# A gated state-space layer and a ternary feed-forward on one core: the prologue and the first units in another order, the dt projection in three row groups

## The reference, cut to what matters

```python
# x: (4, 512, 512); ctx: (4, 512, 256); 512 inner channels, 16 states, dt rank 16
xp  = einsum('bld,ed->bel', ctx, in_proj_w)
u   = silu(causal_conv4(xp, conv_w) + conv_b)
dt_low, B, C = split(einsum('bdl,ed->bel', u, x_proj_w), [16, 32])
dt  = softplus(dt_proj_w @ dt_low + dt_proj_b)
for each time l:                       # 16 states for each channel
    state = state * exp(dt * A) + dt * u * B[l]
    y     = sum_n(state * C[l])
x = x + tanh(g_x) * ((y + D * u) * silu(layernorm(x)))
# feed-forward, 2048 hidden, weights rounded to {-1, 0, 1} by scale 1 / mean|w|
h = silu(bitlinear(layernorm(x), w_gate)) * bitlinear(.., w_up)
x = x + tanh(g_ffn) * bitlinear(h, w_down)
```

## Time and profile before

| | |
|---|---|
| median of 3 runs | 621.03 us (620.51 to 621.07) |
| span of the profiled execution | 617.3 us |
| VectorE busy | 557.0 us, 90% |
| TensorE busy | 520.0 us, 84% |
| ScalarE busy | 519.0 us, 84% |
| GpSimd busy | 508.1 us, 82% |
| mean granted TensorE clock | 0.972 |
| moved by DMA | 64.25 MB |

### The profile page before, as it was taken

How to read it: one execution, slowest core, us unless ns; L and a number is a source line. 1 busy time by engine, 2 the same in 40 slices (tenths; PEclk the granted TensorE clock), 3 DMA queues, 4 the chain that set the end, 5 groups by cost and what they waited for, 6 DMA issues and landing times. The chain is left out here.

```text
span 617.3 us, 9751 instructions
## 1 busy us (share of the span) xinstructions
PE 520.0 (84%) x3254; PEld 363.1 (59%) x3254; DVE 557.0 (90%) x766; ACT 519.0 (84%) x796; POOL 508.1 (82%) x286
## 2 busy tenths in 40 slices
...
DMA packets 30420, 64.25 MB, mean 104 GB/s; under 512 B 3729, under 2 KB 11921, under 8 KB 27554
## 3 DMA queue, kind: packets, MB, share of 16 engines
...
...
## 5 line engine op out<-in xcount | busy, mean ns | idle before, releaser
L850 POOL TENSOR_TENSOR area_s<-area_s,b_bc 128x1024 f32<-128x1024 f32 x117 | 275.0, 2363 | 13.8 <-DVE u_all L1454 9.2
L483 PE MATMUL pY<-ident,area_s 128*128 128x128 f32 x532 | 87.6, 290 | 56.6 <-DVE area_s L1462 56.6
L552 PE MATMUL pG<-wq_gu,area_f 128*128 128x512 fp8e4 x448 | 107.9, 379 | 4.0 <-ACT area_f L1052 2.9
L1454 DVE TENSOR_TENSOR_SCAN area_s<-pA,area_s 128x512 f32<-128x512 f32 x88 | 105.2, 1207 | 5.1 <-ACT pA L1107 4.4
L483 PEld LDWEIGHTS pY<-ident,area_s 128*128 128x128 f32 x532 | 61.6, 146 | 78.0 <-DVE area_s L1462 70.5
L1107 ACT ACTIVATE pA<-dt_all,a_neg 128x512 f32<-128x512 f32 x145 | 97.7, 682 | 10.7 <-DVE area_s L1454 5.9
L842 POOL TENSOR_TENSOR u_all<-u_all 128x1024 f32<-128x1024 f32 x44 | 103.9, 2361 | 0.2 <-DMA u_all<-bc_rows 0.2
L1462 DVE TENSOR_TENSOR area_s<-area_s,pC 128x512 f32<-128x512 f32 x133 | 87.9, 664 | 0.8 <-DVE area_s L1454 0.5
L477 PE MATMUL pC<-ident,xdT 128*128 128x128 f32 x532 | 83.2, 283 | 3.6 <-DVE area_s L1462 2.3
L477 PEld LDWEIGHTS pC<-ident,xdT 128*128 128x128 f32 x532 | 64.3, 143 | 8.9 <-DVE area_s L1462 7.4
L552 PEld LDWEIGHTS pG<-wq_gu,area_f 128*128 128x128 bf16 x448 | 41.7, 98 | 47.1 <-ACT area_f L1052 3.9
...
## 6 DMA issues: line engine op xcount, KB each, us to landing
...
b_bc<-w_gate SPq DMA_DIRECT2D x1, 4096.0 KB, 14.5
dt_all<-x SPq DMA_DIRECT2D x1, 4096.0 KB, 24.8
area_f<-w_up SPq DMA_DIRECT2D x1, 4096.0 KB, 34.2
area_f<-w_down SPq DMA_DIRECT2D x1, 4096.0 KB, 14.4
...
```

Source lines behind the costliest of these rows:

```text
L483: mm = pe.matmul(pY[:, k * P:(k + 1) * P], src[:, k * P:(k + 1) * P], ident[:, :], is_transpose=True, start=(first and k == 0), stop=(last ...
L552: mm = pe.matmul(bank, xqT[t % 2][:, k, :], wq_gu[:, k, m, c * GW:(c + 1) * GW], start=(k == 0), stop=(k == NT - 1))
L850: gp.tensor_tensor(db[c % NDB], du[s % 2].rearrange("p (a l) -> p a l", a=1).to_broadcast([P, CH, L]), b_bc[:, CH * c:CH * c + CH, :], ALU ...
L1454: dve.tensor_tensor_scan(h, at, dbu, 0.0, ALU.mult, ALU.add).then_inc(S["s_scan"], 1)
```

## The change

The dt rows and their weights are laid out three times, at partitions 0, 32 and 96, and B and C move to partitions 64 to 95. `dt_proj(i)` then multiplies only 17 partitions, in the row group of its block. The projections use six banks in place of four. TensorE starts with ten transposes of the identity. All five programs get another order: TensorE makes projections 8 and 9 ahead of `x_proj(0)`, and 12 to 15 in one go. w_gate's chunks go to other engines: GpSimd rounds 0 and 1, VectorE 2 and 3 (`w_round`); ScalarE takes the signs of 0, 2 and 3, the last two in unit 0, and chunk 1 goes through `w_clip` and `w_ternary`. The sums of |w_up| move from VectorE's prologue to ScalarE's unit 0; the further steps of w_up and w_down each stand some states later, up to two signs of w_down in unit 4. The z statistics are handled as 4 and 12 columns. The diff's core:

```diff
-NPROJ = 64
-BROW = 32
+DT_AT = (0, 32, 96)
+BC_AT = 64
...
-px = [pA[:, 0, :], pA[:, 1, :], pC[:, 0, :], pC[:, 1, :]]
-pv = [pG[0][:, :], pG[1][:, :]] + px
...
+px = [pA[:, 0, :], pA[:, 1, :], pC[:, 0, :], pC[:, 1, :], pG[0][:, :], pG[1][:, :]]
+pv = px[4:] + px[:4]
...
-sp.dma_start(w_xp_sb[:, :, 0:RANK], w_xp[:, 0:RANK].rearrange("(t p) n -> p t n", p=P)).then_inc(S["c_w"], 16)
...
-sp.dma_start(w_dt_sb[0:RANK, :], w_dt).then_inc(S["c_w"], 16)
-sp.dma_start(w_dt_sb[RANK:RANK + 1, :], b_dt.rearrange("(a n) -> a n", a=1)).then_inc(S["c_w"], 16)
...
+sp.dma_start(w_xp_sb[:, :, 0:RANK], w_xp[:, 0:RANK].rearrange("(t p) n -> p t n", p=P)).then_inc(S["c_xp"], 16)
...
+for at in DT_AT:
+    sp.dma_start(w_dt_sb[at:at + RANK, :], w_dt).then_inc(S["c_w"], 16)
+    sp.dma_start(w_dt_sb[at + RANK:at + RANK + 1, :], b_dt.rearrange("(a n) -> a n", a=1)).then_inc(S["c_w"], 16)
...
 sp.dma_start(dt_all[:, :, :], x.rearrange("b (t p) f -> p (b t) f", p=P)).then_inc(S["c_x"], 16)
-sp.dma_start(stage[1].rearrange("p (k f) -> p k f", k=NT), w_up.rearrange("(k p) f -> p k f", p=P)).then_inc(S["c_g1"], 16)
-
...
 store_u(1)
+sp.dma_start(stage[1].rearrange("p (k f) -> p k f", k=NT), w_up.rearrange("(k p) f -> p k f", p=P)).then_inc(S["c_g1"], 16)
 store_bc(1)
 store_u(2)
-store_bc(2)
-sp.wait_ge(S["k_p3"], NW)
+sp.wait_ge(S["k_p3"], 1)
 sp.wait_ge(S["c_bst0"], 16)
 load_b(0, (0,))
+store_bc(2)
 store_u(3)
-load_b(0, (1,))
 sp.wait_ge(S["k_conv"], UNITS)
...
 load_z(1)
+sp.wait_ge(S["k_t3"], 1)
+load_b(0, (1,))
+store_bc(3)
 load_x(0)
-load_b(0, (2, 3))
-store_bc(3)
-load_x(1)
-
...
 load_c(0)
+sp.wait_ge(S["k_p3"], 2)
+load_b(0, (2,))
+sp.wait_ge(S["k_p3"], NW - 1)
+load_b(0, (3,))
+load_x(1)
 for b in range(1, BATCH):
...
-sp.wait_ge(S["k_p3"], 2 * NW)
+sp.wait_ge(S["k_p3"], 2 * NW - 1)
 sp.dma_start(stage[2].rearrange("p (k d) -> p k d", k=FK), w_down.rearrange("(k p) d -> p k d", p=P)).then_inc(S["c_g2"], 16)
...
-    past(pe, S["k_tap"], i - 3)
+    past(pe, S["k_tap"], i - 5)
...
-        mm = pe.matmul(px[i % 4], w_in_sb[:, k, t * P:(t + 1) * P], ctx_sb[:, b, k, :], start=(k == 0), stop=(k == KC - 1))
+        mm = pe.matmul(px[i % 6], w_in_sb[:, k, t * P:(t + 1) * P], ctx_sb[:, b, k, :], start=(k == 0), stop=(k == KC - 1))
...
-    if m < 2:
-        pe.wait_ge(S["k_abv"], NW + NW * m)
+    if m == 0:
+        pe.wait_ge(S["k_abv"], NW)
...
-        pe.wait_ge(S["k_abs"], NW)
+        pe.wait_ge(S["k_abs"], NW * m)
...
 def dt_proj(i):
     b, t = i // NT, i % NT
     pe.wait_ge(S["k_rows"], b + 1)
-    if i >= 2:
-
-        pe.wait_ge(S["k_tap"], min(UNITS - NT + i - 1, UNITS))
+    if i < 6:
+        pe.wait_ge(S["k_tap"], UNITS - 4 + i - i % 2)
     past(pe, S["k_dt"], i - 5)
-    pe.matmul(pv[i % 6], w_dt_sb[:, t * P:(t + 1) * P], rows[b], start=True, stop=True).then_inc(S["k_v"], 1)
-
+
+    at = DT_AT[t % 3]
+    pe.matmul(pv[i % 6], w_dt_sb[at:at + RANK + 1, t * P:(t + 1) * P], rows[b][at:at + RANK + 1, :],
+              start=True, stop=True).then_inc(S["k_v"], 1)
+
+pe.wait_ge(S["k_const"], 6)
+for _ in range(WARM):
+    pe.transpose(pT[:, 0:P], ident[:, :], ident[:, :])
 pe.wait_ge(S["c_in"], 16)
-for i in range(2 * NT):
+for i in range(10):
     project(i)
-pe.wait_ge(S["k_const"], 8)
-pe.wait_ge(S["c_w"], 7 * 16)
+pe.wait_ge(S["c_w"], 10 * 16)
+pe.wait_ge(S["k_cp"], 2)
 x_proj(0)
-project(8)
-project(9)
-rows_transpose(0)
 project(10)
 project(11)
-dt_proj(0)
-dt_proj(1)
+rows_transpose(0)
+for i in range(12, UNITS):
+    project(i)
 x_proj(1)
 w_total(0)
-project(12)
-project(13)
+x_proj(2)
 rows_transpose(1)
-project(14)
-project(15)
-x_proj(2)
-dt_proj(2)
-dt_proj(3)
+for i in range(NT):
+    dt_proj(i)
 rows_transpose(2)
-dt_proj(4)
-dt_proj(5)
 x_proj(3)
-for i in range(6, 3 * NT):
+for i in range(NT, 3 * NT):
     dt_proj(i)
 rows_transpose(3)
 for i in range(3 * NT, UNITS):
...
+gp.wait_ge(S["k_const"], 5)
...
+for i, at in enumerate(DT_AT):
+    gp.wait_ge(S["k_const"], 6 + i)
...
+gp.wait_ge(S["k_const"], 10)
...
+gp.wait_ge(S["c_xp"], 16)
+for at in DT_AT[1:]:
+    gp.tensor_copy(w_xp_sb[:, :, at:at + RANK], w_xp_sb[:, :, 0:RANK]).then_inc(S["k_cp"], 1)
...
-conv_sums(0, 10)
+conv_sums(0, 12)
...
-conv_sums(10, 12)
+conv_sums(12, UNITS)
...
-conv_sums(12, 14)
-w_round(2)
-conv_sums(14, UNITS)
-w_round(3)
-w_clip(3)
+w_clip(1)
...
+def z_roots(first, last, done):
...
+    gp.wait_ge(S["k_ag"], last)
...
+z_roots(0, NT, 0)
...
-gp.wait_ge(S["k_st"], 2 * UNITS)
...
+z_roots(NT, UNITS, 4)
...
-        if n in (1, 3, 5, 7):
+        if s == 0 and n == CH * pooled(s)[0] + 2:
+            times_c(s, 0)
+            times_b(s, NDB)
+            times_b(s, NDB + 1)
+        if n in (1, 3, 5, 7) and (s > 0 or n > 3):
...
-        if n == CH * pooled(s)[0] + 2:
+        if s > 0 and n == CH * pooled(s)[0] + 2:
...
-    act.wait_ge(S["k_p1"], NW * m + c + 1)
+    if m == 0 and c > 1:
+        act.wait_ge(S["k_p2"], c - 1)
+    else:
+        act.wait_ge(S["k_p1"], 2 + NW * (m - 1) + c + 1 if m else c + 1)
...
     if i:
         silu(i - 2)
         silu(i - 1)
-act.wait_ge(S["k_const"], 9)
-rows_out(0)
 conv_start(8)
 conv_start(9)
 silu(6)
 silu(7)
-act.wait_ge(S["c_w"], 7 * 16)
-act.activation(tgate[:, :], g_raw[:, :], ACT.Tanh).then_inc(S["k_a"], 1)
+act.wait_ge(S["k_const"], 10)
+rows_out(0)
 conv_start(10)
 conv_start(11)
 silu(8)
 silu(9)
-rows_out(1)
+act.wait_ge(S["c_w"], 10 * 16)
+act.activation(tgate[:, :], g_raw[:, :], ACT.Tanh).then_inc(S["k_a"], 1)
 conv_start(12)
 conv_start(13)
 silu(10)
 silu(11)
 conv_start(14)
 conv_start(15)
+rows_out(1)
+silu(12)
+silu(13)
 w_sign(0, 0)
 rows_out(2)
-silu(12)
-silu(13)
-w_sign(0, 1)
 silu(14)
 silu(15)
-w_sign(0, 2)
-for i in range(3):
+for i in range(NT):
     softplus(i)
 rows_out(3)
-for i in range(3, UNITS):
+for i in range(NT, UNITS):
     softplus(i)
 act.wait_ge(S["k_dt"], UNITS)
 act.wait_ge(S["k_a"], 2)
...
+        act.wait_ge(S["k_zs"], 8)
...
-    if s == 0 and n >= 4 and n % 2 == 0 and n < 4 + 2 * NW:
-        w_scale(1, n // 2 - 2)
-    if s == 1 and n % 2 == 0 and n < 2 * NW:
-        w_sign(1, n // 2)
-    if s == 2 and n % 2 == 1 and n < 1 + 2 * NW:
-        if n == 1:
+    if s == 0 and n in (0, 1):
+        w_sign(0, 2 + n)
+    if s == 0 and n in (5, 7, 11, 13):
+        if n == 5:
+            act.wait_ge(S["c_g1"], 16)
+        w_abs(1, (5, 7, 11, 13).index(n))
+    if s == 1 and n in (2, 4, 6, 8):
+        w_scale(1, n // 2 - 1)
+    if s == 1 and n in (10, 13, 15) or s == 2 and n == 1:
+        w_sign(1, (10, 13, 15, 1).index(n))
+    if s == 2 and n in (11, 13, 15) or s == 3 and n == 1:
+        if n == 11:
...
-        w_abs(2, n // 2)
-    if s == 3 and n % 2 == 0 and n < 2 * NW:
-        w_scale(2, n // 2)
-    if s == 3 and n in (8, 10, 12):
-        w_sign(2, 7 - n // 2)
+        w_abs(2, (11, 13, 15, 1).index(n))
+    if s == 3 and n in (4, 6, 8, 10):
+        w_scale(2, n // 2 - 2)
+    if s == 3 and n in (13, 15):
+        w_sign(2, 3 - n // 15)
...
-    if s == PLAIN and n == 3:
...
-        w_sign(2, 0)
+    if s == PLAIN and n in (3, 7):
...
+        w_sign(2, 1 - n // 7)
...
-    dve.tensor_scalar(ternary(0, c), raw(0, c), -MAGIC, None, ALU.add, saturate=False).then_inc(S["k_p3"], 1)
+    dve.tensor_scalar(ternary(0, c), raw(0, c), -MAGIC, None, ALU.add, saturate=False).then_inc(S["k_t3"], 1)
...
+def w_round(c):
+    dve.wait_ge(S["k_wm"], 3)
+    dve.tensor_scalar(raw(0, c), raw(0, c), w_inv[:, 0:1], MAGIC, ALU.mult, ALU.add).then_inc(S["k_p2"], 1)
...
+def z_moments(first, last):
+    dve.wait_ge(S["k_st"], last)
+    for i in range(first, last):
+        dve.bn_aggr(z_mv[:, i, :], st_x[:, i, :]).then_inc(S["k_ag"], 1)
...
 taps(8)
 rows_copy(0)
 w_abs(0, 2)
+taps(10)
 w_abs(0, 3)
+taps(12)
 w_means(0)
-taps(10)
-for i in range(3):
+taps(14)
+for i in range(NT):
     x_stats(i)
-taps(12)
+z_moments(0, NT)
 rows_copy(1)
-x_stats(3)
-x_stats(4)
-taps(14)
+w_round(2)
+w_round(3)
+for i in range(NT, 2 * NT):
+    x_stats(i)
 rows_copy(2)
-for i in range(5, UNITS):
+w_ternary(1)
+for i in range(2 * NT, UNITS):
     x_stats(i)
-dve.wait_ge(S["k_st"], UNITS)
-for i in range(UNITS):
-    dve.bn_aggr(z_mv[:, i, :], st_x[:, i, :]).then_inc(S["k_st"], 1)
-w_ternary(3)
-w_abs(1, 0)
-w_abs(1, 1)
 rows_copy(3)
-w_abs(1, 2)
-w_abs(1, 3)
+z_moments(NT, UNITS)
...
-    if s == 0 and n == 1:
+    if s == 1 and n == 1:
...
-    if s == 2 and n == 14:
+    if s == 3 and n == 3:
```

61 lines of the change are left out of this document (30 added, 31 removed).

## The result

| | before | after |
|---|---|---|
| median of 12 runs | 620.61 us (619.23 to 621.34) | 624.30 us (620.63 to 625.41) |
| span of the profiled execution | 617.3 us | 618.8 us |
| first exponential X | 69.22 | 65.93 |
| w_down issued | 111.85 | 128.94 |
| unit 4, first scan | 178.00 | 178.49 |

The ratio after to before is 1.0059, 95% interval 1.0046 to 1.0071: slower by 0.6%, and outside the range given. The execution profiled of after took 620.63 us, 1.8 above its span, and is the fastest of the twelve. So the two traces explain 1.5 of the 3.7 us between the medians; the rest is taken up in the experiments.

A forecast was written before the change was run, and what follows sets the result against it. VectorE and GpSimd are dense from unit 5 on, so only its start could shift. 64.3 + 62.7 + 14.6 + 54.7 put the first gate SiLU 1.0 us earlier: span 616.3, time 620.0 us, range 617.0 to 623.4.

The forecast's parts named there:

- G: ScalarE's first SiLU of a gate product, in unit 4: forecast at 196.3 against 197.26, 1.0 us earlier.
- The last SiLU of u at 52.0: Prologue: after VectorE's and GpSimd's work from 23.5, ScalarE's last SiLU of u ends at 52.0, 2.0 us earlier.
- X = 64.3: End of the prologue: ScalarE's first exponential at 52.0 + 12.0 + 0.3 = 64.3, 4.9 us earlier.
- rival D: TensorE slows down ahead of x_proj(3), which takes up to 3.4 us more: 621.7 to 623.4 us; chance 0.20.
- The row groups: Twelve dt projections overlap in distinct row groups, passing in 5 to 7 us, so ScalarE's softplus sets the pace.
- Rival C: No overlap of row groups in the dt projections: first exponential at 68.7, 4.4 later, time 624.4 us, slower; chance 0.15.
- Unit 0, and w_down issued at X + 62.9: ScalarE's list: 28.1 us in unit 0 without a wait; w_down issued at 127.2, where it was 111.85.
- w_down's 14.6: From issuing w_down at 127.2, its transfer takes 14.4, and its first |w| sum comes at 141.6.
- From w_down to G, 54.7: ScalarE from w_down's first sum to the first gate SiLU: 38.5 plus 16.1 us, with waits gone.
- Behind G everything keeps its distance: After unit 4's first gate SiLU the 1.0 us gain goes unchanged to the end: span 617.3 to 616.3.
- The base: Whole kernel: profiled span 617.3 us, median 621.03, and the 3.7 us between them carried over.
- Rival B: ScalarE keeps up in units 0 to 4, so 3.7 us reach the end: 617.3 us, faster; chance 0.15.

The follow-up runs named there:

- the gate filling: After with 32 more transposes of the identity on TensorE in unit 4, around its wait ahead of the first gate product: 622.39 us, ratio 1.0034.
- the version with early u(3) and later z SiLUs: After with u(3) loaded ahead of w_down and z SiLUs 2 and 3 eight states later: 619.26 us; with 21 transposes ahead of x_proj(3) too, 619.22 us.
- second measurement: The changed kernel, after, measured again with no edit: 622.90 us, ratio to before 1.0036.

## Why the prediction was wrong, step by step

The sum was G = X + 62.7 + 14.6 + 54.7. The trace gives 65.93 + 63.0 + 14.8 + 56.1 = 199.8, against 196.3. Of the 3.5 us, 1.0 came back behind G, and the median lies 1.8 further above its span than I had carried over: 620.0 + 3.5 - 1.0 + 1.8 = 624.3. Two steps of the sum failed: the cost of x_proj(3), and the path from w_down to G. Then TensorE's clock at the first gate product had no term.

- **The last SiLU of u at 52.0**: 52.09. The walk of VectorE and GpSimd held. VectorE's two roundings took 2.65 each beside GpSimd's (`49.08 5.30 x2`), where I had put 1.1 and 0.3 for alternation; VectorE had the slack for it, as it waited 3.02 for the first exponential.
- **X = 64.3**: 65.93, 1.6 late. The failing term is x_proj(3) at 3.7. It took 5.40, which is rival D, with its reason and with half its price of 3.4. I had given it 0.20, although the gap from 49.3 to 52.1 was in my own walk. That a late X goes through to the end shows in the profile of after with the gate filling: X is 1.5 later there than in after's own, and so is the end. (In the version with early u(3) and later z SiLUs it was not so: what the filling won at X was lost in unit 0.) The Trainium skill (TensorE: Matmul & The Clock Gate, section on why this matters) warns of idle gaps between bursts of matmuls, and the row agrees.
- **The row groups**: right. ScalarE sets the pace of the softplus. Rival C was mispriced: without overlap X is 11.8 later and the time 13 us longer, not 4.4, because the price was taken from projections over 128 rows at full clock.
- **Unit 0, and w_down issued at X + 62.9**: unit 1 at X + 28.9 (forecast 28.8), w_down at X + 63.0. VectorE waits 1.83 and 0.78 us for exponentials 7 and 9, as written; for 15 the trace has no wait. ScalarE's list gave the right length up to here.
- **w_down's 14.6**: 14.8.
- **From w_down to G, 54.7**: 56.1. This step failed in kind. I had moved w_down's issue by 15 us and asked only who waits for w_down. Behind it on SyncE's queue stands the load of u(3): GpSimd, with no slack, waited 4.24 for it, and 2.7 of that reached VectorE. ScalarE, for which I had forecast no waits in unit 3, waited 1.91 for TensorE there (at 167.81).
- **Behind G everything keeps its distance**: from G to the end 419.0, before 420.0, so 1.0 came back in the profiled run. It does not always. In the profiles of after and its versions the first gate product took 1.90 or 3.60. With the first it is 419.0 to 419.2 us from G to the end, with the second 419.9 to 420.5. G itself comes 2.45 behind the start of the product with the first and 3.3 with the second. From the szT product of unit 3 to that of unit 4 it is 32.3 to 32.4 us and 33.9 to 34.6. So the lower clock in this one place goes with about 2 us more. I had no term for it.
- **The base**: I carried 3.7 us from span to median, where a time lies 1.8 above its own span; the rest was the place of that execution among the runs. For after the median lies 5.5 above the profiled span.

Rival B was wrong: ScalarE did not keep up, as VectorE's waits for it and w_down's issue at X + 63.0 show.

Two different edits each take the loss away. One is to fill both places ahead of which the new order leaves TensorE idle: the ratio to before falls from 1.0036 (second measurement) to 1.0008, with intervals that just touch. Neither filling alone did it (1.0031 and 1.0034). That each run meets the lower clock in one place or the other would fit, but no trace shows it, with one profile for each version. The other edit is to move two z SiLUs to where ScalarE waits: 3.3 us, measured together with after, although the profiled run of that version met the lower clock in both places (6.17 and 3.59). So the lower clock alone does not make after slower than before. That version loses most of the extra length of unit 3: 29.8 us, where after has 32.3 and before 28.7. The early load of u(3) shortens the same stretch. X is 1.3 later there than in after, and that is more than made up in units 1 and 3.

The early load of u(3) alone takes 1.6 us from the same stretch and 0.3 from the time, in a profile in which the gate product again met the lower clock. Left open are how the loss of a typical run divides between the clock and unit 3, and what after would take with both fillings and an early u(3), or with both fillings and the later z SiLUs alone.
